# A linear attention stage on TensorE: the next tile's keys and values go directly behind gate and up, contexts and states behind them

## The reference, cut to what matters

```
q = relu(x @ Wq.T + bq);  k = relu(x @ Wk.T + bk);  v = x @ Wv.T + bv      # x is the layer norm of the stream
kv     = einsum('bnhd,bnhp->bhdp', k, v)         # the "state" of a head, per batch row of 64 positions
denom  = max(einsum('bnhd,bhd->bnh', q, k.sum(1)), 1e-6)
out    = einsum('bnhd,bhdp->bnhp', q, kv) / denom # the "context"
x      = x + layernorm(out + x_normed) * gamma + beta
# then
x      = x + (silu(xn @ Wgate) * (xn @ Wup)) @ Wdown        # hidden 768, xn is the layer norm of the stream
```

## Time and profile before

| | |
|---|---|
| median of 3 runs | 2112.57 us |
| profiled execution, its own time | 2111.39 us |
| its span, first to last instruction | 2109.7 us |
| TensorE matmul busy | 2039.2 us |
| VectorE busy | 1205.8 us |
| ScalarE busy | 1123.7 us |
| GpSimd busy | 498.2 us |
| mean granted TensorE clock | 0.988 |

### The profile page before, as it was taken

The page is one execution under the profiler, slowest core; times in us unless marked ns, Lnnn a source line. Parts: engine busy times, 40 slices in busy tenths (PEclk is TensorE's granted clock), DMA queues, the critical chain, the costliest instruction groups (busy, mean ns, idle before and its releaser), DMA issues. The chain is left out here.

```text
span 2109.7 us, 46357 instructions
## 1 busy us (share of the span) xinstructions
PE 2039.2 (97%) x18833; PEld 1831.1 (87%) x18833; DVE 1205.8 (57%) x3622; ACT 1123.7 (53%) x2556; POOL 498.2 (24%) x411
## 2 busy tenths in 40 slices
PE   6999999999999999699899999999999999999998
PEld 5999999999999999366778888789999999999998
DVE  5656565655565655567668898734947733242411
ACT  4556555656565655333358777643544444444443
POOL 0000020000000000123311222143444444444444
PEclk9999999999999999899999999999999999999999
DMA  4000200000000000100031110100110101101000
GB/s 150 22 16 22 76 22 17 21 16 22 16 22 16 21 17 2 45 1 1 1 87 42 32 32 22 42 1 1 61 41 1 41 1 41 41 1 40 1 11 31
DMA packets 48787, 57.81 MB, mean 27 GB/s; under 512 B 6529, under 2 KB 40129, under 8 KB 48449
## 3 DMA queue, kind: packets, MB, share of 16 engines
q1 hardware_dynamic: 48576, 54.85, 8.2%
HBM read 46.72 MB, written 2.10 MB: 23 GB/s over the span
## 5 line engine op out<-in xcount | busy, mean ns | idle before, releaser
L933 POOL TENSOR_TENSOR right_h<-right_hr,right_h 128x512 fp32r<-128x512 f32 x256 | 341.4, 1334 | 429.5 <-ACT right_hr L1245 429.5
L1244 ACT ACTIVATE right_h<-bank,dec_b 128x512 fp32r<-128x512 f32 x256 | 176.2, 688 | 401.7 <-PE bank L83 370.8
L83 PE MATMUL bank<-lat_wv,lat_kv_t 128*128 128x256 f32 (+1 forms) x1728 | 260.3, 302 | 5.4 <-DVE lat_wv L2271 5.4
L83 PE MATMUL bank<-lat_kv_t,lat_qk 128*128 128x320 f32 x1536 | 254.8, 315 | 1.9 <-ACT lat_p L2206 1.9
L83 PEld LDWEIGHTS bank<-lat_kv_t,lat_qk 128*128 128x128 f32 x1536 | 226.3, 188 | 9.8 <-issue 2.1
L83 PEld LDWEIGHTS bank<-lat_wv,lat_kv_t 128*128 128x128 f32 x1728 | 224.4, 191 | 11.6 <-DVE lat_wv L2271 5.6
L2206 ACT ACTIVATE lat_p<-bank,lat_neg_max 128x320 f32<-128x320 f32 x256 | 136.3, 532 | 174.1 <-DVE lat_neg_max L2321 174.1
L83 PE MATMUL bank<-dec_xt,dec_lo 128*128 128x512 f32 x512 | 202.0, 395 | 0.0
L1245 ACT ACTIVATE right_hr<-bank,dec_b 128x512 f32<-128x512 f32 x256 | 174.5, 682 | 0.0
L1725 POOL TENSOR_TENSOR lat_rs_rstdc<-lat_rs_varc,lat_rs_halfc 128x4 f32<-128x4 f32 x16 | 16.2, 1015 | 642.5 <-DVE lat_rs_varc L1717 642.5
L1102 PE MATMUL bank<-dec_hi,right_h 128*128 128x256 f32 x1024 | 163.4, 281 | 0.5 <-POOL right_h L933 0.5
(11 more groups left out here) (322 smaller groups left out, 3906.2 us busy)
## 6 DMA issues: line engine op xcount, KB each, us to landing
raw_w<-in_L_ffn_W SPq DMA_DIRECT2D x16, 1024.0 KB, 6.4
lat_ctx_raw<-in_ctx SPq DMA_DIRECT2D x16, 512.0 KB, 4.0
right_ctx_raw<-in_ctx_turned SPq DMA_DIRECT2D x16, 512.0 KB, 3.7
lat_kv_t<-lat_lt SPq DMA_DIRECT2D x32, 128.0 KB, 2.1
out_x<-x_sb SPq DMA_DIRECT2D x4, 512.0 KB, 2.9
x_sb<-in_x SPq DMA_DIRECT2D x1, 1792.0 KB, 14.9
lat_xl_now<-lat_xl SPq DMA_DIRECT2D x7, 256.0 KB, 4.7
ahead_room<-in_L_xattn_Wq SPq DMA_DIRECT2D x1, 1024.0 KB, 7.0
```

Source lines behind the costliest of these rows:

```text
L83: mm = pe.matmul(out, lhs(a, k), rhs(b, k), start=first and k == 0 and n == 0, stop=last and k == KD - 1 and n == 2)
L933: pool.tensor_tensor(h[:, g % 2, 1, :], hr[:, g % 2, :], h[:, g % 2, 0, :].bitcast(F32), ALU.subtract).then_inc(h_lo, 1)
L1244: act.activation(h[:, n % 2, 0, :], h_bank[n % 2][:, :], ACT.Relu, bias=bias).then_inc(h_hi, 1)
```

## The change

`keys_values` of the next tile moves up in TensorE's program within a pass, ahead of `contexts` and `states`. Nothing is added or removed, and the programs of the other engines stay as they are.

```
--- before.py
+++ after.py
@@ -420,12 +420,12 @@
                 for i in range(PER + 1):
                     if c >= 1:
                         gate_up(c - 1, i)
+                    if i + 1 < PER:
+                        keys_values(PER * c + i + 1)
                     if i >= 1:
                         contexts(PER * c + i - 1)
                     if i < PER:
                         states(PER * c + i)
-                    if i + 1 < PER:
-                        keys_values(PER * c + i + 1)
                 if c >= 1:
                     gate_up(c - 1, NH - 1)
                 if c + 1 < NCH:
```

## The result

The changed kernel takes 2126.08 us, median of 7 runs (2118.89 to 2127.73), against 2113.31 us for the kernel before (7 runs, 2111.95 to 2114.54). That is 12.8 us more, ratio 1.0054 with a 95% interval of 1.0042 to 1.0066. The forecast was 2119.0 in 2115 to 2124, so the sign was right and the time lies above the range. Two of the seven runs (2118.89 and 2119.19) lie on the forecast, the other five between 2125.3 and 2127.7. A second set of five runs gave 2125.65 to 2127.38.

What follows compares the result with a forecast made beforehand. TensorE, busy 97% of the span, was taken as the bound, its chunk ends waiting on VectorE. 4.9 + 0.5 + 0.8 + 0.8 = +7.0 us on 2111.39 gives 2118.4; 2119.0 was stated, range 2115 to 2124.

Steps and rivals of the forecast that it cites:

- Chunk 0, +4.9: In chunk 0 the moved keys and values wait for VectorE's bank read, so the last contexts come 4.9 us late.
- the replay: Step-by-step start times worked out for chunk 0 in the new order, ending with the last contexts at 883.8, before 878.91.
- the ring: In chunk 0, keys and values, contexts and states, and VectorE's bank read wait on each other; 5.67 us a round.
- Chunks 1 to 3, +0.5, +0.8, +0.8: VectorE's backlog makes the ends of chunks 1, 2 and 3 later by 0.5, 0.8 and 0.8 us.
- TensorE's own cost of a pass: In chunks 1 to 3, 5.93 us a pass, taken as unchanged by the new order (0, between -0.26 and +0.24).
- What follows the stage is only shifted: Behind the stage, the later program was claimed to move in time only, adding nothing to the sum.
- a microsecond or so: At the chunk ends, how much the length of the slow-clock stretches could shift.
- Rival A: The clock falls in chunk 0, doubling TensorE's work in two rounds: +4.6 us, 2123.6; chance 0.17.
- Rival B: Chunks 1 to 3 absorb their delays, only 4.9 us stays: 2116.9; chance 0.12.
- C: In pass 3 of chunks 1 to 3 `y` clears GpSimd's `hidden_low`: +2.0 us in all, 2114; chance 0.09.
- The chance for slower, 0.82: Whole kernel: chance 0.82 of slower, starting at 2116.8 us; within 0.2% 0.15, faster 0.03.
- The stall before `turn_ffn`: In chunk 0 TensorE's 5.75 us idle there, waiting for VectorE's chain, was claimed to stay unchanged.

Runs made afterwards that it cites:

- c0_only: Against the kernel before, the block moved only in chunk 0, chunks 1 to 3 keeping the old order; 2121.8 us, ratio 1.0042.
- dve_follows: Changed kernel with VectorE's read of the keys and values also moved ahead of its contexts and states; 2118.1 us, 1.0021 against the kernel before.
- shift_1_7: Kernel before with one extra pair of unused matmuls (1.7 us) ahead of the first keys and values; 2112.9 us, ratio 0.9999.
- shift_5: Kernel before with three extra pairs of unused matmuls (5.1 us) ahead of the first keys and values; 2119.8 us, ratio 1.0030.
- before_tail_5_1: Kernel before with three extra matmul pairs (5.1 us) behind the first gate and up of the stage's last part; 2123.0 us, ratio 1.0046.
- fill_c0: Changed kernel with an extra pair of unused matmuls behind states in passes 0 to 2 of chunk 0; 2126.6 us, 1.0062 against the kernel before.
- after_plus_1_7: Changed kernel with one extra pair of unused matmuls (1.7 us) ahead of the first keys and values; 2128.8 us.
- after_tail_1_7: Changed kernel with one extra matmul pair (1.7 us) behind the first gate and up of the stage's last part; 2123.4 us.
- after_mid_1_7: Changed kernel with one extra pair of unused matmuls (1.7 us) at the start of chunk 2's passes; 2125.5 us.
- shift_3_4: Kernel before with two extra pairs of unused matmuls (3.4 us) ahead of the first keys and values; 2115.9 us, ratio 1.0014.

## Why the prediction was wrong

- **Chunk 0, +4.9: right, in mechanism and size.** 20.98 - 16.14 = 4.84. The starts of the keys and values lie 2.83, 7.16 and 12.82 us behind the first; the replay had 2.83, 7.16 and 12.83. c0_only shows that it is the moved block there, dve_follows that it is VectorE's place for the read that closes the ring.
- **Chunks 1 to 3, +0.5, +0.8, +0.8: right.** Chunk 2 is 0.79 longer, chunk 3 0.66 at its last contexts and 0.84 at the start of `down` (33.25 against 32.41), and in chunk 1 the contexts of pass 4 wait 0.46. The waits stand where they were placed (0.46, 0.68 and 0.54 before the contexts of pass 4). TensorE's own cost of a pass did not change, as taken: the passes of chunk 2 are 965.87 - 959.93 = 5.94 against 5.93. The schedule's sum is 4.84 + 0.5 + 0.79 + 0.84 = 7.0, as forecast. The two lowest runs (2118.9 and 2119.2) lie near it, but they have no trace, and their mean clock of 0.986 is also below before's 0.988.
- **"What follows the stage is only shifted": wrong,** and this is the step that failed. I gave the length of the slow stretches "a microsecond or so" and put nothing into the sum for the number of them. The traces show that a program shifted by a few us gets other clock falls. Against before, in the profiled execution: end of chunk 2 +1.60, last `down` +1.48 and decoder +4.24, less about 1.0 for slow stretches in chunks 1 and 3 that were shorter. Another +1.32 lies ahead of the changed code (the first keys and values at 864.09 for 862.77) and has nothing to do with the change: where the program ahead is the same, this start lies anywhere from 862.77 to 865.3 in the traces. Together that is 7.6 of the span's 14.6. The kernels with before's order and only a displacement show each of the three losses: the first in shift_1_7, the second in shift_1_7, shift_5 and before_tail_5_1, the third in shift_5 and, less by 1.2, in before_tail_5_1.
- **Rival A (the clock falls in the ring): its time came closest, its mechanism was not the cause.** In the changed kernel the rounds are at full speed; only the last states and contexts of chunk 0 are not. fill_c0 keeps the clock up there and takes as long. The Trainium skill, "TensorE: Matmul & The Clock Gate", section "A second HAM failure mode: psum-queue depth-cycling", tells of another kernel whose micro-idles between groups of matmuls make the clock oscillate, which carried over to this one would put the loss into these rounds. The traces agree in part: after_plus_1_7 has such a fall (+1.6) and after_tail_1_7 too (+2.3), the changed kernel's own two traces have none and lose the time all the same.
- **Rival B and C: wrong.** Chunks 1 to 3 did not absorb their delays, and `y` of pass 3 takes its 1.38 again.
- **The chance for slower, 0.82, was borne out,** but nearly half of the 12.8 us came by a way that the forecast had left out; the range was too narrow because B and A alone set its ends. The stall before `turn_ffn` was 2.99 and not 5.75, since TensorE did the turning, the queries and the next keys and values at 1.2 GHz in that gap: the slow stretch there was covered. `turn_ffn` came 0.5 later behind the first keys and values than in the replay (35.15 for 29.80 + 4.84), and it took 0.4 less itself.

What is open: why the falls at the end of chunk 2 come at some displacements and not at others (1.7 brings it, 3.4, 5.1 and 6.8 do not, and after_mid_1_7 kept it), and why before's own place is one with few of them. Nor is the size of the displacement all that counts: c0_only delays what follows chunk 0 by 4.84 and has the fall at the end of chunk 2 (19.75), shift_5 delays it by 5.1 and has not (18.05). And it is not the distance from the start of the span: the two traces of the changed kernel reach the first keys and values at 864.09 and 865.29 us and have the same losses. Which falls come is therefore shown to change with a mere displacement, but these runs give no rule for where they come.

## What to carry to other kernels

When an instruction moves ahead in one engine's queue, find the release that it waits for in the other engine's queue: if that release stands behind work which the moved instruction now blocks, a ring closes, and its round (here 5.67 us summed from rows, 5.66 measured) sets the pace, or costs nothing where other work in a pass is longer (here 5.93). A wait that a ring saves on one engine is only worth something if the other engine's order moves with it. And where TensorE idles for 2 to 3 us between stages, compare a change of a few microseconds with kernels that are merely displaced by as much: here 1.7 to 6.8 us of added work made from 0 to 10.6 us. A single trace can be of an untypical run, so look at where its time lies among the others first.

## What the runs showed that was not expected

- 1.7 us of extra matmuls cost 0.15 us (2112.9 against 2112.8), and 5.1 us cost 7 to 10.6, depending on their place: the difference is low granted clock in stages that were not touched. Extra work of 1.7 us at the tail made the changed kernel's median 2.9 us lower (five runs each; one of them took 2127.7 and lies above).
- A gap of 2.25 us, and one of 2.92 us, is followed by full speed in shift_3_4 and by 1.2 GHz in shift_1_7, whose programs differ by one pair of matmuls ahead of chunk 0. The price was 1.5 to 1.7 us each.
- The decoder, the same program in all kernels, took 1043.1 to 1049.7 us in their traces.
